# Two transformer-like layers on one core: the first routing weights fetched in halves, their table written from two queues, and the second routing's maxima at another place

## The reference

```python
x = x + attention(xn, ...) + moe(xn, w_gate, w1_e, w3_e, w2_e, w1_s, w3_s, w2_s)

# attention: at each of the 512 positions the 8 batches attend to each other, 16 heads of 8
attn = softmax(q @ k.T * 8 ** -0.5); out = (attn @ v) @ out_w.T + out_b

# moe: 16 experts of 64 hidden units in 4 groups, plus one shared expert of 128
scores = sigmoid(x @ w_gate.T)          # 16 per token
# keep the 2 best groups (by the sum of their 2 best), then the 4 best experts, normalise
combine = chosen_scores / (sum + 1e-6)  # zero for the 12 other experts
routed = sum_e combine[:, e] * (silu(x @ w1_e.T) * (x @ w3_e.T)) @ w2_e
shared = (silu(x @ w1_s.T) * (x @ w3_s.T)) @ w2_s.T
```

## Time and profile before

| | us |
|---|---|
| median of 3 runs | 365.11 |
| lowest, highest | 364.57, 365.88 |
| the profiled execution | 366.06 |
| its span, first to last instruction | 364.2 |
| layer 1 starts on TensorE, about | 160.6 |
| PE, DVE, ACT, POOL busy | 307.7, 311.2, 186.4, 239.0 |

### The profile page before, as it was taken

How to read it: one execution, slowest core, us unless ns; L and a number is a source line. 1 busy time by engine, 2 the same in 40 slices (tenths; PEclk the granted TensorE clock), 3 DMA queues, 4 the chain that set the end, 5 groups by cost and what they waited for, 6 DMA issues and landing times.

```text
span 364.2 us, 4906 instructions
## 1 busy us (share of the span) xinstructions
PE 307.7 (84%) x1371; PEld 218.2 (60%) x1371; DVE 311.2 (85%) x825; ACT 186.4 (51%) x507; POOL 239.0 (66%) x152
## 2 busy tenths in 40 slices
PE   0569876989899887685988999999989999998993
PEld 0336664768677776563655755656657566565662
DVE  5995899987977868947989899898998989989792
ACT  3345756878678578491342632536236361352611
POOL 3185587655736531107779868889888998889651
PEclk9987999999999999699899999999999999999999
DMA  4690000000000000019633324225343252335000
GB/s 138 175 276 1 2 0 1 3 1 0 3 0 3 0 0 3 0 33 169 161 92 80 114 62 121 81 67 137 116 100 99 76 137 73 101 106 132 3 29 29
DMA packets 21311, 24.81 MB, mean 68 GB/s; under 512 B 2428, under 2 KB 12068, under 8 KB 21284
## 3 DMA queue, kind: packets, MB, share of 16 engines
q1 hardware_dynamic: 20336, 24.09, 25.0%
q10 hardware_dynamic: 820, 0.39, 0.4%
q0 software_dynamic: 128, 0.01, 0.0%
HBM read 22.13 MB, written 2.36 MB: 67 GB/s over the span
## 4 chain that ended last, share of the span: by engine, by line
DVE 37%; PE 25%; issue 15%; POOL 12%; ACT 7%; DMA 3%; SPq 1%; ACTq 0%; DVEq 0%; POOLq 0%
PE Q L917 11%; POOL prod_qk L856 8%; PE VN L917 7%; PE T L917 3%; DVE att L1549 3%; DVE rope_b L1326 3%; DVE rope_a L1324 3%; DVE hid L1587 3%; DVE sgc L1574 3%; POOL prod_pv L866 2%; PE T L913 2%; DVE bst L1167 2%; DVE attn L1356 2%; ACT L750 1%; DMA cw<-comb_table 1%
## 5 line engine op out<-in xcount | busy, mean ns | idle before, releaser
L856 POOL TENSOR_TENSOR prod_qk<-qkv 128x1024 f32<-128x1024 f32 x32 | 76.3, 2395 | 17.0 <-DVE above L1419 15.2
L866 POOL TENSOR_TENSOR prod_pv<-prob,qkv 128x1024 f32<-128x1024 f32 x32 | 69.6, 2195 | 18.5 <-DVE att L1549 17.0
L917 PE MATMUL VN<-hid,w 128*128 128x512 f32 x144 | 74.6, 599 | 1.5 <-DVE hid L1587 1.5
L917 PE MATMUL Q<-xT_hi,w_hi 128*128 128x512 f32 x72 | 52.1, 724 | 0.2 <-ACT sg L750 0.2
L1587 DVE TENSOR_TENSOR hid<-T,sgc 128x512 f32<-128x512 f32 x64 | 43.4, 679 | 0.0
L1535 DVE TENSOR_REDUCE scr<-prod_qk 128x128 f32<-128x1024 f32 x32 | 38.8, 1213 | 5.0 <-POOL prod_qk L856 4.9
L917 PE MATMUL Q<-bias,ones 128*128 128x400 f32 (+1 forms) x64 | 30.3, 474 | 15.1 <-ACT v_ext L638 7.1
L917 PE MATMUL T<-xT_hi,w_hi 128*128 128x512 f32 x72 | 30.8, 428 | 9.4 <-DVE hid L1587 9.3
L1549 DVE TENSOR_REDUCE att<-prod_pv 128x128 f32<-128x1024 f32 x32 | 38.3, 1197 | 0.0
L750 ACT ACTIVATE VN<-Q 128x512 f32<-128x512 f32 x32 | 18.6, 582 | 36.7 <-PE Q L917 29.1
L750 ACT ACTIVATE ND<-Q 128x512 f32<-128x512 f32 x32 | 18.6, 582 | 35.7 <-PE Q L917 24.7
(11 more groups left out here) (176 smaller groups left out, 747.9 us busy)
## 6 DMA issues: line engine op xcount, KB each, us to landing
cw<-comb_table SPq DMA_DIRECT2D x64, 256.0 KB, 4.5
out_x<-fin SPq DMA_DIRECT2D x8, 256.0 KB, 4.5
x<-in_x SPq DMA_DIRECT2D x2, 256.0 KB, 3.0
wraw<-in_w1T SPq DMA_DIRECT2D x1, 512.0 KB, 4.1
w3raw<-in_w3T SPq DMA_DIRECT2D x1, 512.0 KB, 4.7
w<-in_w2T SPq DMA_DIRECT2D x1, 512.0 KB, 5.7
rope_s<-in_c_sin ACTq DMA_DIRECT2D x1, 256.0 KB, 4.9
rope_c<-in_c_cos SPq DMA_DIRECT2D x1, 256.0 KB, 5.4
```

Source lines behind the costliest of these rows:

```text
L856: pool.tensor_tensor(prod_qk[:, t % 2], bc(qkv2[:, TH * half + t, j, 0:D], 1, NB), qkv2[:, :, j, D:2 * D], ALU.mult).then_inc(qk_prod, 1)
L866: pool.tensor_tensor(prod_pv[:, t % 2].rearrange("p (h e) b -> p b h e", e=HD), bc(prob[:, t].rearrange("p h b -> p b h"), 3, HD), qkv2[:, ...
L917: return pe.matmul(o, lhsT, rhs, start=start, stop=stop)
```

## The change

It has three parts.

1. The table's first half is written from two queues: SP writes the blocks of k = 0, GpSimd those of k = 1. GpSimd waits for `combT_ready` for that, ahead of its first product of layer 1, and has a semaphore of its own, `comb_kept_pool`. SP waits for both before it reads. The second half of the table is still written by SP alone, and its count is lower (96 rather than 128).
2. For the first slot's first quarter, the two transfers of 256 KB become four of 128 KB (`spread_first`), the two for e = 0 (slice 1) first, with the semaphore `ld_cw_one`, then the two for e = 1 (slice 2), with `ld_cw[0]`. VectorE waits for the former at slice 1, for the latter at slice 2.
3. The second routing's maxima move from slice k = 1, ahead of its `hid`, to slice k = 5, behind its `hid`.

```diff
+        ld_cw_one = sem("ld_cw_one")
+        comb_kept_pool = sem("comb_kept_pool")
...
             def keep_comb(half):
                 sp.wait_ge(combT_ready, half + 1)
                 settle(sp)
-                for k in range(2):
+                for k in range(1 if half == 0 else 2):
                     for b in range(2):
                         sp.dma_start(table[:, half, :, 2 * k + b, :].rearrange("e j p -> j e p"),
                                      combT[NJ * NE * b:NJ * NE * (b + 1), half, k, :]).then_inc(comb_kept, 16)
+
+            def spread_first():
+                for e in range(2):
+                    for r in range(2):
+                        src = table[2 * e + r, 0, 0].rearrange("b p -> (b p)")
+                        sp.dma_start(cw[64 * r:64 * r + 64, 0, e], src.partition_broadcast(64))\
+                            .then_inc((ld_cw_one, ld_cw[0])[e], 16)
...
                     keep_comb(1)
-                    sp.wait_ge(comb_kept, 128)
+                    sp.wait_ge(comb_kept, 96)
...
             keep_comb(0)
-            sp.wait_ge(comb_kept, 64)
-            for q in range(NPART):
+            sp.wait_ge(comb_kept, 32)
+            sp.wait_ge(comb_kept_pool, 32)
+            spread_first()
+            for q in range(1, NPART):
                 spread(0, q)
...
+            pool.wait_ge(combT_ready, 1)
+            settle(pool)
+            for b in range(2):
+                pool.dma_start(table[:, 0, :, 2 + b, :].rearrange("e j p -> j e p"),
+                               combT[NJ * NE * b:NJ * NE * (b + 1), 0, 1, :]).then_inc(comb_kept_pool, 16)
             pool.wait_ge(l1_kept, NT)
             pool.wait_ge(r_step, R_ABOVE)
...
-                    if r % 2 == 0:
+                    if n == 0 and r == 0:
+                        dve.wait_ge(ld_cw_one, 32)
+                    if r % 2 == (1 if n == 0 and r < 2 else 0):
                         dve.wait_ge(ld_cw[r // 2], 32 * (n + 1))
...
-                if k == 1:
-                    route_top(1)
...
                 if k == 0:
                     route_limits(1)
                     route_masked(1)
                     assert r_done[0] == R_MASKED
+                if k == 5:
+                    route_top(1)
```

## The result

| | before | changed |
|---|---|---|
| median of 6 runs each, us | 365.72 | 361.76 |
| lowest, highest, us | 364.57, 366.06 | 361.42, 362.51 |
| ratio, 95% interval | | 0.9897 (0.988 to 0.9914) |
| span of the profiled execution, us | 364.2 | 359.6 |
| end of the copy of `combT` on ScalarE (combT_ready), us | 157.33 | 155.95 |

A forecast was written before the change was run, and what follows sets the result against it. VectorE was taken to pace the first slot, with at most 3.58 us of removable idling. Earlier weights and moved maxima, walked together, gave 3.4 us: 361.7 us from the median 365.11, range 361.1 to 362.5, chance 0.66.

The forecast's parts named there:

- The walk on VectorE: First slot, step by step on VectorE: first sgc at 165.3, eighth slice's sgc at 180.7 instead of 184.07, 3.4 us ahead.
- The table from two queues: Table writes before layer 1: GpSimd's write takes 3.0 us, landing at 161.1 (160.2 to 162.8), against 161.34 before.
- The halves: First slice's cw weights in 128 KB transfers: landing 3.3 us after issue, pair there at 165.2 (163.8 to 167.7), before 166.95.
- the full transfer queue hides the two extra issues: SP's cw fetches: the two additional issues cost SP 1.3 us, which the full transfer queue covers.
- a sign of being wrong: Listed as wrong: GpSimd write landing after 161.5, sgc waiting for its quarter of cw, or hole reopening in second slot.
- The maxima: Sixteen maxima and a memset, 1.42 us, leave the place before hid and cover the exponential's wait; alone 2.0 us saved.
- fixed path: Row maximum to slice 7's sgc, through GpSimd's subtraction and ScalarE's table loads, exponential and gate: held behind VectorE's 1.43 us wait.
- the price of another one: If TensorE's clock falls again, the last gate ends at 181.1 instead of 180.1, costing 0.4 us at most.
- Late weights: Rival: GpSimd's writes and the halves land late, first sgc stays at 167.04, only the maxima count; 2.0 us saved, 363.1; chance 0.20.
- Nothing comes through: Rival: VectorE's lead is eaten in a later slot by something unshifted, such as the cw stream; 365.1 us; chance 0.09.
- Slower: Rival: GpSimd's two table writes come very late and hold SP's fetches; 2.5 us slower, 367.6; chance 0.05.

The follow-up runs named there:

- e3: Changed kernel with all four table writes on SP again, halves and moved maxima kept: 362.46 us, ratio 0.9922 to the kernel before.
- e4: Changed kernel with the first quarter of cw fetched in two transfers of 256 KB again: 363.30 us, ratio 0.9936 to the kernel before.
- e9: Changed kernel with the table written by SP alone in two transfers instead of four: 362.21 us, ratio 0.9896 to the kernel before.
- e2: Changed kernel with the maxima put back ahead of the second slice's hid: 363.76 us, ratio 0.9954 to the kernel before.
- e5: Changed kernel with the maxima behind slice 3's hid, ahead of the row maximum: 362.76 us, ratio 0.9921 to the kernel before.
- e7: Kernel before plus 14 extra matmuls while TensorE waits ahead of slice 3's up product: 364.00 us, ratio 0.996 to the kernel before.
- e1: Kernel before with only the maxima moved, behind the sixth slice's hid: 363.77 us, ratio 0.9953 to the kernel before.
- e8: Changed kernel with five of eight parts of the second routing's replacements moved behind slice 14's hid: 360.77 us, ratio 0.9866 to the kernel before.
- e6: Kernel before with only the maxima moved, behind slice 3's hid, ahead of the row maximum: 363.79 us, ratio 0.9953 to the kernel before.

## Why the prediction was right, point by point

**The time.** Forecast 361.7, measured 361.76. That the two agree to 0.06 us is luck: by the medians it is a gain of 3.96 from 365.72, where 3.4 from 365.11 was forecast. In the part that was changed the gain is 3.2. The walk on VectorE ended with the eighth slice's sgc 180.7 - 157.3 = 23.4 us after combT_ready; it came after 23.53. At no sgc before it was the walk more than 0.5 us off.

**The table from two queues: mis-sized.** The term had GpSimd's write landing 3.0 us after its issue. It took 2.23; its second issue, though, came 157.27 - 155.95 = 1.32 us after combT_ready and not 0.8, since GpSimd let 0.6 us pass between the signal and its first issue. Together the table is whole 0.46 us sooner than before, where the forecast had 161.34 - 161.1 = 0.24, and e3 shows where that counts: at the second quarter of cw, 0.53 us. The Trainium skill's 0.4 us between the two first bytes ("DMA: Bandwidth & Descriptors", § Latency and other measured facts) has the right sign, and the measured difference, from issue to landing, is smaller: 2.23 us on GpSimd's queue, 2.09 on SP's.

**The halves: right, with one false step.** They landed after 3.0 us (3.3 forecast), ahead of the masking, and scores then waited for GpSimd's product as forecast. But that the full transfer queue hides the two extra issues did not hold. The last piece of the second quarter was issued 162.78 - 159.57 = 3.2 us after the first fetch, where it had been 2.0, and VectorE waited 0.31 us for it. I had called the place tight, and had named an sgc that waits for its quarter of cw as a sign of being wrong; that sign came. The 8.9 us from the first fetch to this landing were taken over from before as they stood; they became 169.26 - 159.57 = 9.69. e4 and e9 show both ends of it: without the extra issues, or with the table 0.7 us sooner, that wait is gone.

**The maxima: right in size, wrong in cause.** Alone they were to give 2.0 us, and gave 1.98. I put the 0.36 us down to a late TensorE, but all of the 1.43 to a "fixed path" from the row maximum. The path without disturbance takes 4.4 us (e2, e5) and leaves 0.83 us of hole, not 0.36 + 1.43. The walk itself had it at 4.4 (175.7 to 180.1), though before the same path took 5.5; that difference was the sign. The other 0.96 us of the two holes, and 0.2 us of small delays in the slices before them (two steps of 0.71 and 0.70 where others take 0.60), came with the fall of TensorE's clock after its 3.90 us of idling; e7 measures both as 1.19. The prediction saw that fall and gave 0.4 us as the price of another one, but did not ask what the first had cost: ScalarE cannot load the exponential's table until the late gate of slice 6 is through. The walk had the right sum because it let both holes go, whatever had made them.

So the 3.2 us are made up like this: 1.4 for the earlier start (the first scores begin 8.94 us after combT_ready, before 10.32), less 0.3 at the second quarter; 1.2 for the clock; 0.83 for the cover. That is 3.1. Moving the maxima alone brings the last two (2.0, e1); the earlier weights alone bring the first two (1.4 + 1.2 = 2.6, e2 2.64), since either shortens TensorE's idling; for the maxima alone the clock's share is less sure, as e1's idle time was short partly by luck. This is why the two don't add up. Taken out of the changed kernel one at a time, the three parts cost only 0.58 (maxima, e2), 0.53 (second queue, e3) and 0.56 us (halves, e4): each time the other two still keep the clock up.

**The rivals.** Late weights: the GpSimd write took 2.23 us, near the lower bound of 2.09, and the halves 3.0, near theirs of 2.8, so the case did not come; e1 is its figure (363.77, a gain of 1.9; forecast 363.1 on a median of 365.1, a gain of 2.0). One argument against it was misread: the GpSimd loads did not run beside the heaviest load traffic, which came from 16 to 24 us at 305 GB/s, while the first 8 us had 120 and 193. Nothing comes through: the lead was 3.21 us at the eighth slice and 3.22 at the end. Slower: the slow GpSimd write did not occur; VectorE was idle while it was prepared, as forecast.

## What to carry to other kernels

Before putting an idle time down to the instruction named as its releaser, follow that one engine further back: here VectorE's wait for ScalarE was TensorE's low clock, made by TensorE's own wait a few slices earlier, and filler matmuls alone won 1.19 us, over a third of what the change won. Work that nobody needs soon belongs right behind the step that starts a long path through other engines; e8 shows that the next wait can take most of that gain. When two edits remove the same idle time, cost them together and not one by one.

## What the runs showed of the hardware

TensorE's granted clock fell to 0.5 (1.2 GHz) in the slices behind idle times of 3.90 and 3.00 us and not behind 1.13, 2.07 and 2.54 us (the kernel before, e6; e1, e4, e2). With 14 matmuls in the first of these idle times it stayed at 1.00 (e7). I had expected a write from GpSimd's queue to be slower than it was: 2.23 us from issue to landing for 32 KB, 0.14 more than on SP, with 0.6 us between the semaphore and its first issue on the idle engine. And 128 KB to 64 partitions landed 3.0 us after issue where 256 KB took 4.1.
